# Turning x for the q projection: PE transposes replaced by a DRAM round trip and 32x32 block transposes, from the fourth tile on

## The chip, the cores and the metric

One core of one Trainium2 chip runs the kernel. Its engines are named as in the profile: PE (TensorE, with its weight loads PEld), DVE (VectorE), ACT (ScalarE), POOL (GpSimd) and SP (SyncE, which here only issues DMAs). Each engine works through its own list of instructions in order and waits on semaphores. The metric is the time of one execution on the device in microseconds; less is better.

## The reference

Everything is float32. There are 32 tiles of 128 tokens with 512 features each; a tile attends only to its own 128 context rows (the image part of the context; the text part is empty here). The second half is a feed-forward layer.

```python
def attention_block(x, ctx):                       # x, ctx: (32, 128, 512), 16 heads of 32
    xn = (x - mean(x)) / sqrt(var(x) + 1e-5)
    q = rms_norm(xn @ q_w.T + q_b, norm_q_w)
    k = rms_norm(ctx @ k_img_w.T + k_img_b, norm_k_img_w)
    v = ctx @ v_img_w.T + v_img_b
    a = softmax(q @ k.T / sqrt(32)) @ v            # per head
    return x + tanh(g_xattn) * (a @ o_w.T + o_b)

def feed_forward(x):
    h = normalise(x)
    y = square(relu(h @ up_w)) @ down_w + (h @ expert_w) * sum(top2(h @ gate_w))
    return x + tanh(g_ffn) * (layer_norm(y) * gamma + beta)
```

## The kernel before

The kernel has two phases in one block of instructions: attention, which writes its result tile by tile to a DRAM scratch, and the feed-forward layer, which works on groups of four tiles. The change is in the first.

**Precision.** A float32 product is done on PE as three products of a high and a low part. So every stationary and moving operand is split: ACT copies it to a rounded high part (`cT_hi`, `xnT_hi`, `aT_hi`), and DVE or POOL subtracts that from the original to get the low part (`cT_lo`, `xnT_lo`, `aT_lo`). The helper `mm3` then issues three matmuls for each of the four slices of 128 features. `xnT_hi` and `xnT_lo` are the transposed normalised x: 128 features of a slice on the partitions, tokens along the columns.

**Slots.** `run` calls one function `slot(s, par)` on every engine, for s = -1 to 30, mostly from a hardware loop of two slots per turn (`par` is the parity, which picks one of two buffers); `drain` does the rest. A slot works on four tiles at once: s (scores and softmax), n = s+1 (projections of k, q, v), a = s-1 (turning the probabilities, multiplying with v), o = s-2 (output projection and residual).

**PE's order in a slot** (L367): scores of s; k projection (`BK`) and q projection (`BQ`) of n, the latter behind `dv_xT`, the count of finished `xnT_lo`; three groups of probability transposes; the output projection of o; the fourth group; the turn of kf; the values (L343), whose last quarter waits for ACT's `pT` of group 3; `turn_x` of tile s+2 (L305), four 128x128 transposes of `xn` into the PSUM bank 7 (`BTX`); the turn of qf; the v projection (`BV`). `BTX`, `BQ` and the output projection's `BO` are the same bank, which is why `turn_x` waits for `dv_qb` and `dv_x2`.

**DVE's order in a slot** (L508): `bias_v` (vb = v projection + bias, L496), `lo_xT` (xnT_lo from `BTX`, L444 in the profile), four `maxima` (L466), reciprocals (`inverse`) between ACT's exponentials, kb, `normalise` of tile s+2 (xn, L456), qb, kf, `residual_sum`, the statistics of a later x, `split_values` (aT_lo); in slots 24 to 27 also the statistics of a feed-forward tile.

**ACT's order in a slot** (L690): the exponentials in four groups (L641), each behind its maxima; squares of k and q; the copies `pT` of the four groups (L619); qf; kT; cT_hi; aT_hi; qT; `hi_xT` (xnT_hi from `BTX`); in slots 2 to 21 the high part of a piece of the feed-forward weights.

**POOL's order in a slot** (L825): in slots 3 to 22 first the low part of such a piece, released by vb (L988); four divides of the probabilities (L801); small square roots; the residual plus bias (L823); cT_lo (L788); in slots 24 to 27 the normalisation of a feed-forward tile (L1223).

**SP's order in a slot** (L245): load of xres; load of xin for tile s+4, behind xn of tile s+2; load of cin for s+4, behind ACT's cT_hi and POOL's cT_lo; store of x2; stores and load of weight pieces. All go to one DMA queue.

**The round trip that exists already.** In the feed-forward phase x is turned without PE: `out_blocks` (L1417) stores a tile to DRAM in runs of 32 columns (128 bytes), dealt so that each 32x32 block lies where it must be, `in_blocks` (L1421) loads it back row by row, and `turn_blocks` (L1154, STREAM_TRANSPOSE) transposes each 32x32 block on DVE. There four tiles are stored and loaded one after the other.

Of the kernel before, what the change touches and what calls it, by code (L numbers as in the profile page):

```python
# [5 lines left out]
F32 = mybir.dt.float32  # L6
# [5 lines left out]
P = 128  # L12
D = 512
KT = D // P
# [9 lines left out]
def flamingo_layer(nc, t, out):  # L24
# [8 lines left out]

    x2_dram = nc.dram_tensor("x2_scratch", [NB, P, D], F32, kind="Internal").ap()
    xn_dram = nc.dram_tensor("xn_scratch", [2 * GB, P, D], F32, kind="Internal").ap()
    ring_dram = nc.dram_tensor("ring_scratch", [t["down"].shape[1] // D + KT, 2, P, D], F32, kind="Internal").ap()

    def at_least(eng, sem, value, apart=False):
# [9 lines left out]
    with ExitStack() as whole:  # L48
        def sem(name):
            return whole.enter_context(nc.semaphore(name))  # L50

        def sb(ctx, name, shape, dt=F32):
            return ctx.enter_context(nc.sbuf_tensor(name, shape, dt))
# [40 lines left out]
        with ExitStack() as ctx:  # L94
# [6 lines left out]
            kf, qf = sb(ctx, "kf", [P, D]), sb(ctx, "qf", [P, D])  # L101
            kb, qb = sb(ctx, "kb", [P, D]), sb(ctx, "qb", [P, D])
            xn = sb(ctx, "xn", [P, D])
            bv = sb(ctx, "bv", [P, D])
            tgbo = sb(ctx, "tgbo", [P, D])
            vb = [sb(ctx, f"vb{n}", [P, D]) for n in range(2)]
# [18 lines left out]

            ld_w = [[sem(f"ld_w{n}{k}") for k in range(2)] for n in range(4)]
            ld_bk, ld_bq, ld_bv, ld_bo, ld_n = (sem("ld_" + n) for n in ("bk", "bq", "bv", "bo", "norms"))
            ld_x, ld_c, ld_r = ([sem(f"{s}{n}") for n in range(2)] for s in ("ld_x", "ld_c", "ld_r"))
            wh, wl, wl_late, cst = sem("weights_hi"), sem("weights_lo"), sem("late_weights_lo"), sem("row_consts")
            pe_K, pe_Q, pe_Tx, pe_TP, pe_PV, pe_Tk, pe_Tq, pe_S, pe_O = (  # L130
# [24 lines left out]

            def is_slot(b, n):
                return isinstance(b, int) and b == n

            def probs_taken(eng, a, g):

# [32 lines left out]
            def strip(h):  # L193

                return slice(h * HD, (h + 1) * HD)

            def by_strip(a):

# [13 lines left out]
            def _(sp):  # L212
# [32 lines left out]
                def slot(s, par):  # L245
                    a, n, o = s - 1, s + 1, s - 2
                    if has(a):
                        at_least(sp, dv_x2, a - 1, apart=True)
                        load(a, 1 - par, t["x"], xres, ld_r)
                    if has(s + 4):  # L250
                        at_least(sp, dv_xn, s + 3, apart=True)
                        load(s + 4, par, t["x"], xin, ld_x)
                        at_least(sp, ac_c, s + 3, apart=True)
                        at_least(sp, po_c, s + 3, apart=True)
                        load(s + 4, par, t["ctxT"], cin, ld_c)
                    if has(o):
                        at_least(sp, dv_x2, o + 1, apart=True)
                        sp.dma_start(x2_dram[o], x2[par][:, :]).then_inc(st_x2[par], DMA)
                    if ff.has_half(s - 3):
                        ff.q_store(sp, s - 3, 1 - par)  # L260
                    if ff.has_half(s - 1):
                        ff.q_load(sp, s - 1, 1 - par)
                    if is_slot(s, NB - 9):
                        for m in range(2):
                            sp.wait_ge(st_x2[m], GB // 2 * DMA)
                    if isinstance(s, int) and NB - 9 <= s < NB - 4:
                        ff.load_first(sp, s - (NB - 9))
# [19 lines left out]
            def _(pe):  # L287
# [16 lines left out]

                def turn_x(b):  # L305
                    at_least(pe, dv_qb, b)
                    at_least(pe, dv_x2, b - 3)
                    at_least(pe, dv_xn, b + 1)
                    turn(xn, BTX, pe_Tx)

# [56 lines left out]
                def slot(s, par):  # L367
# [3 lines left out]
                    if has(n):  # L371
                        at_least(pe, po_c, n + 1)
                        mm3(pe, BK, cT[1 - par], wk, ready=split_weight(n, 0)).then_inc(pe_K, 1)
                        at_least(pe, dv_xT, n + 1)
                        mm3(pe, BQ, xT, wq, ready=split_weight(n, 1)).then_inc(pe_Q, 1)
                    if is_slot(s, 0):
                        pe.wait_ge(dv_vb, 1)
# [19 lines left out]
                    if has(a):  # L397
                        for g in range(NG):
                            values(a, 1 - par, g)
                    if has(n + 1) and not is_slot(n, 0):  # L400
                        turn_x(n + 1)
                    if has(n):
                        at_least(pe, ac_qf, n + 1)
# [38 lines left out]
            def _(dve):  # L442
# [9 lines left out]

                def normalise(b, par):
                    at_least(dve, po_rs, b + 1)
                    at_least(dve, pe_Tx, b)
                    dve.tensor_scalar(xn[:, :], xin[par][:, :], mv[:, 0:1], rstd[:, 0:1], ALU.subtract, ALU.mult).then_inc(dv_xn, 1)  # L456

                def lo_xT(b):
                    at_least(dve, ac_xT, b + 1)
                    sub(xnT_lo[:, :], BTX, xnT_hi[:, :]).then_inc(dv_xT, 1)  # L460

                def maxima(b, g):

# [44 lines left out]
                def slot(s, par):  # L508
# [54 lines left out]
                        stats(s + 3, 1 - par)  # L563
                    if has(a):
                        split_values(a)
                    if starting:
                        stats(2, 0)
                    if is_slot(s, 0):
# [48 lines left out]
            def _(act):  # L617
# [1 line left out]
                    return act.activation(dst, src, ACT.Copy)  # L619

                def hi_xT(b):
                    at_least(act, pe_Tx, b + 1)
                    copy(xnT_hi[:, :], BTX).then_inc(ac_xT, 1)

                def hi_ctx(b, par):
                    at_least(act, ld_c[par], parity_count(b, par))
# [1271 lines left out]
```

## Time and profile before

| | |
|---|---|
| median of 3 runs | 1374.52 us (1373.98 to 1375.23) |
| the profiled execution | 1372.42 us |
| its span | 1370.6 us |
| attention: PE alone on the chain of waits | 61.9 to 537 us |
| feed-forward phase | from about 560 us to the end |
| instructions | 27962 |

The profile is of one execution. Its page gives the busy time of each engine, the span in 40 slices, the DMA queues, the chain of work that ended last, the costliest groups of instructions and the DMA issues. The timeline lists instructions by start time, with the idle time before one and what ended it in brackets. An instruction's recorded duration can overlap the next one's start: the distance of two starts tells what an instruction costs on its engine. A stage table gives each engine's busy time within a stretch.

### The profile page before, as it was taken

How to read it: one execution, taken by the hardware profiler on the slowest of the kernel's cores; microseconds unless marked ns; L12 is line 12 of the kernel's file. 1: busy time of each engine (PE TensorE's matmuls, PEld its weight loads, DVE VectorE, ACT ScalarE, POOL GpSimd, SP SyncE). 2: the span in 40 equal slices, each digit the busy share in tenths (PEclk: the TensorE clock that was granted, in tenths of full speed). 3: DMA queues.
4: the chain of work that ended last, by engine and by line, in shares of the span. 5: the costliest groups of instructions: out<-in, count | busy, mean ns of one | idle time of the engine just before them, and what ended most of it. 6: DMA issues, size and time to landing. Idle time of an engine off the chain costs nothing.

```text
span 1370.6 us, 27962 instructions
## 1 busy us (share of the span) xinstructions
PE 1334.5 (97%) x9264; PEld 1139.9 (83%) x9264; DVE 893.7 (65%) x1739; ACT 614.1 (45%) x1891; POOL 524.2 (38%) x671
## 2 busy tenths in 40 slices
PE   6899999999999999999999999999999999999996
PEld 5688888888888888898888888888888888888884
DVE  5555555555555655887776785775775776776764
ACT  4777777777777777532312212322213113223210
POOL 3566666666665776433131131140140140240211
PEclk9999999999999999999999999999999999999998
DMA  6133333333333311448549449458368468367541
GB/s 232 55 99 109 107 107 107 107 107 111 120 113 96 104 63 41 160 140 204 180 147 253 144 154 252 130 154 254 125 164 250 138 168 249 116 177 222 174 144 36
DMA packets 215091, 199.15 MB, mean 145 GB/s; under 512 B 126321, under 2 KB 126449, under 8 KB 215025
## 3 DMA queue, kind: packets, MB, share of 16 engines
q1 hardware_dynamic: 182768, 139.57, 34.9%
q10 hardware_dynamic: 32256, 58.73, 12.8%
q8 instruction: 37, 0.61, 0.2%
q14 instruction: 30, 0.24, 0.1%
HBM read 156.32 MB, written 41.94 MB: 145 GB/s over the span
## 4 chain that ended last, share of the span: by engine, by line
PE 81%; issue 8%; DVE 5%; POOL 1%; ACT 1%; ACTq 0%; DVEq 0%; POOLq 0%
PE bank L75 16%; PE bank L77 16%; PE bank L76 16%; PE wide L76 7%; PE wide L77 7%; PE wide L75 7%; PE bank L340 4%; PE bank L302 3%; PE wide L318 2%; PE wide L352 2%; ACT prob L641 1%; DVE c L1298 1%; POOL yrstd L1790 1%; PE wide L1491 1%; PE wide L1488 1%
## 5 line engine op out<-in xcount | busy, mean ns | idle before, releaser
L1565 ACT ACTIVATE hT_hi<-c 128x512 fp32r<-128x512 f32 x128 | 79.9, 631 | 402.9 <-PE wide L77 210.1
L641 ACT ACTIVATE prob<-wide,nmx 128x128 f32<-128x128 f32 x512 | 182.3, 403 | 103.4 <-DVE nmx L466 100.1
L1797 POOL TENSOR_TENSOR pair<-pair,beta 128x512 f32<-128x512 f32 x28 | 37.5, 1339 | 451.3 <-DMA pair<-x_scratch 451.3
L76 PE MATMUL wide<-wo_lo,hT_hi 128*128 128x512 f32 x512 | 203.3, 397 | 0.0
L77 PE MATMUL wide<-wo_hi,hT_lo 128*128 128x512 f32 x512 | 201.9, 394 | 0.0
L75 PE MATMUL wide<-wo_hi,hT_hi 128*128 128x512 f32 x512 | 201.5, 394 | 0.0
L801 POOL TENSOR_TENSOR prob<-prob,rr 128x512 f32<-128x512 f32 x128 | 138.3, 1081 | 94.9 <-DVE rr L474 92.0
L1643 DVE TENSOR_TENSOR hT_lo<-c,hT_hi 128x512 fp32r<-128x512 f32 x128 | 99.2, 795 | 75.6 <-ACT hT_hi L1565 74.8
L641 ACT ACTIVATION_READ_ACCUMULATOR prob<-wide,nmx 128x1 f32 x512 | 124.0, 242 | 0.0
L77 PEld LDWEIGHTS wide<-wo_hi,hT_lo 128*128 128x128 f32 x512 | 96.1, 188 | 22.7
L75 PEld LDWEIGHTS wide<-wo_hi,hT_hi 128*128 128x128 f32 x512 | 96.2, 188 | 21.5
L76 PEld LDWEIGHTS wide<-wo_lo,hT_hi 128*128 128x128 f32 x512 | 96.1, 188 | 20.6
L75 PE MATMUL bank<-wq_hi,up_hi 128*128 128x256 f32 x384 | 108.6, 283 | 3.1 <-DVE c L1271 3.1
L76 PE MATMUL bank<-wq_lo,up_hi 128*128 128x256 f32 x384 | 107.9, 281 | 0.0
L77 PE MATMUL bank<-wq_hi,up_lo 128*128 128x256 f32 x384 | 107.7, 281 | 0.0
L1298 DVE SCALAR_TENSOR_TENSOR c<-c 128x512 f32<-128x512 f32 x128 | 83.8, 696 | 0.0
L77 PE MATMUL bank<-wv_hi,up_lo 128*128 128x256 f32 x288 | 81.2, 282 | 0.0
L76 PE MATMUL bank<-wv_lo,up_hi 128*128 128x256 f32 x288 | 80.9, 281 | 0.0
L75 PE MATMUL bank<-wv_hi,up_hi 128*128 128x256 f32 x288 | 80.8, 280 | 0.0
L466 DVE TENSOR_REDUCE nmx<-wide 128x4 f32<-128x512 f32 x128 | 79.3, 682 | 0.0
L619 ACT ACTIVATE pT<-bank 128x512 f32<-128x512 f32 x122 | 75.0, 669 | 5.4 <-PE bank L340 4.6
L75 PEld LDWEIGHTS bank<-wq_hi,up_hi 128*128 128x128 f32 x384 | 72.4, 189 | 4.4 <-DVE c L1271 4.4
(226 smaller groups left out, 3548.7 us busy)
## 6 DMA issues: line engine op xcount, KB each, us to landing
wo_hi<-ring_scratch ACTq DMA_DIRECT2D x110, 256.0 KB, 3.7
wo_lo<-ring_scratch ACTq DMA_DIRECT2D x110, 256.0 KB, 4.5
wo_hi<-ring_scratch SPq DMA_DIRECT2D x46, 256.0 KB, 2.7
wo_lo<-ring_scratch SPq DMA_DIRECT2D x46, 256.0 KB, 2.9
fx<-x_scratch SPq DMA_DIRECT2D x36, 256.0 KB
xin<-in_x SPq DMA_DIRECT2D x32, 256.0 KB, 2.6
cin<-in_ctxT SPq DMA_DIRECT2D x32, 256.0 KB, 2.8
xres<-in_x SPq DMA_DIRECT2D x32, 256.0 KB, 4.0
```

Of the source, the lines that this page charges most:

```text
L75: eng.matmul(dst, ah, bh, start=first and k == 0, stop=False)
L76: eng.matmul(dst, ah, bl, start=False, stop=False)
L77: mm = eng.matmul(dst, al, bh, start=False, stop=last and k == n - 1)
L302: mm = pe.transpose(cols(dst, k), cols(src, k), ident[:, :])
L340: mm = pe.transpose(cols(dst, h), prob[par][:, g, h * P:(h + 1) * P], ident[:, :])
L466: dve.tensor_reduce(nmx[:, g * HG:(g + 1) * HG], bank[g].rearrange("p (h k) -> p h k", h=HG), AX.X, ALU.max, negate=True).then_inc(dv_mx, 1)
L619: return act.activation(dst, src, ACT.Copy)
L641: i = act.activation(prob[par][:, g, h * P:(h + 1) * P], cols(bank[g], h), ACT.Exp, bias=nmx[:, n:n + 1], scale=1.0, accum_out=rs[:, n:n + 1])
L801: pool.tensor_tensor(p, p, r, ALU.mult).then_inc(po_p, 1)
L1298: dve.scalar_tensor_tensor(out=cc[:, m, :], in0=cc[:, m, :], scalar=0.0, in1=cc[:, m, :], op0=ALU.max, op1=ALU.mult).then_inc(dv_h, 1)
L1565: return act.activation(dst, src, ACT.Copy)
L1643: dve.tensor_tensor(ff.hT_lo[i % 2][:, :], ff.c[i // 2 % 2][:, i % 2, :], ff.hT_hi[i % 2][:, :].bitcast(F32), ALU.subtract).then_inc(ff.dv ...
```

## The change

From tile 3 on (`XD = 3`, `dealt(b)`), PE no longer turns xn. Instead:

- SP stores `xn` to the scratch `xd_dram` in runs of 32 columns, in front of the load of the next xin, and after the store has landed (`st_xd`) loads the rows back to `x_dealt`, in front of the load of cin.
- DVE transposes the 32x32 blocks of `x_dealt` into `x_turned` (`turn_blocks`), behind `split_values`.
- ACT's `hi_xT` and DVE's `lo_xT` read `x_turned` from SBUF instead of the bank, block by block, and write `xnT_hi` and `xnT_lo` in token order: runs of 32 read side by side, written 4 floats apart (`by_blocks`, `in_order`).
- `normalise` waits until the store of the tile before has landed instead of for PE's turn. The wait on `dv_x2` that guarded the bank in `turn_x` now stands in front of the q projection. ACT's `hi_xT` waits for PE's last q projection.

```diff
+    xd_dram = nc.dram_tensor("xd_scratch", [2, P, D], F32, kind="Internal").ap()
...
+            x_dealt, x_turned = sb(ctx, "x_dealt", [P, D]), sb(ctx, "x_turned", [P, D])
...
+            XD = 3
+            def dealt(b):
+                return not isinstance(b, int) or XD <= b < NB
+            def dealt_count(b):
+                return (b - (XD - 1)) * DMA
...
+            def by_blocks(a):
+                return a[:, :].rearrange("p (c k b) -> p k c b", c=KT, k=KT)
+            def in_order(a):
+                return a[:, :].rearrange("p (k b c) -> p k c b", c=KT, k=KT)
...
 # SP, slot
+                    if dealt(s + 2):
+                        at_least(sp, dv_xn, s + 3, apart=True)
+                        there = xd_dram[par].rearrange("(i b) (c k d) -> (b c) k i d", i=HG, c=KT, k=KT)
+                        sp.dma_start(there, xn[:, :].rearrange("p (k i d) -> p k i d", k=KT, i=HG)).then_inc(st_xd, DMA)
                     if has(s + 4):
                         at_least(sp, dv_xn, s + 3, apart=True)
                         load(s + 4, par, t["x"], xin, ld_x)
+                    if dealt(s + 2):
+                        at_least(sp, st_xd, dealt_count(s + 2), apart=True)
+                        at_least(sp, dv_xt, s + 2 - XD, apart=True)
+                        sp.dma_start(x_dealt[:, :], xd_dram[par]).then_inc(ld_xd, DMA)
+                    if has(s + 4):
                         at_least(sp, ac_c, s + 3, apart=True)
                         at_least(sp, po_c, s + 3, apart=True)
                         load(s + 4, par, t["ctxT"], cin, ld_c)
...
 # PE
                 def turn_x(b):
                     at_least(pe, dv_qb, b)
-                    at_least(pe, dv_x2, b - 3)
                     at_least(pe, dv_xn, b + 1)
                     turn(xn, BTX, pe_Tx)
...
                         at_least(pe, dv_xT, n + 1)
+                        at_least(pe, dv_x2, o)
                         mm3(pe, BQ, xT, wq, ready=split_weight(n, 1)).then_inc(pe_Q, 1)
...
-                    if has(n + 1) and not is_slot(n, 0):
+                    if is_slot(s, 0):
                         turn_x(n + 1)
...
 # DVE
                 def normalise(b, par):
                     at_least(dve, po_rs, b + 1)
-                    at_least(dve, pe_Tx, b)
+                    at_least(dve, pe_Tx, min(b, XD) if isinstance(b, int) else XD)
+                    if not isinstance(b, int) or b > XD:
+                        at_least(dve, st_xd, dealt_count(b - 1), apart=True)
...
                 def lo_xT(b):
                     at_least(dve, ac_xT, b + 1)
-                    sub(xnT_lo[:, :], BTX, xnT_hi[:, :]).then_inc(dv_xT, 1)
+                    if dealt(b):
+                        sub(in_order(xnT_lo), by_blocks(x_turned), in_order(xnT_hi)).then_inc(dv_xT, 1)
+                    else:
+                        sub(xnT_lo[:, :], BTX, xnT_hi[:, :]).then_inc(dv_xT, 1)
+
+                def turn_blocks(b):
+                    at_least(dve, ld_xd, dealt_count(b))
+                    at_least(dve, ac_xT, b)
+                    dve.transpose(x_turned[:, :], x_dealt[:, :]).then_inc(dv_xt, 1)
...
                     if has(a):
                         split_values(a)
+                    if dealt(n + 1):
+                        turn_blocks(n + 1)
...
 # ACT
                 def hi_xT(b):
-                    at_least(act, pe_Tx, b + 1)
-                    copy(xnT_hi[:, :], BTX).then_inc(ac_xT, 1)
+                    if dealt(b):
+                        at_least(act, dv_xt, b - (XD - 1))
+                        at_least(act, pe_Q, b)
+                        copy(in_order(xnT_hi), by_blocks(x_turned)).then_inc(ac_xT, 1)
+                    else:
+                        at_least(act, pe_Tx, b + 1)
+                        copy(xnT_hi[:, :], BTX).then_inc(ac_xT, 1)
```

## Rows read from the trace of the kernel before

**Rows 1.** The page's part 1: busy us, share of the span, instructions.
```profile
PE 1334.5 (97%) x9264; PEld 1139.9 (83%) x9264; DVE 893.7 (65%) x1739; ACT 614.1 (45%) x1891; POOL 524.2 (38%) x671
```

**Rows 2.** Stage table, one slot: length, busy per engine, PEclk, DMA share, GB/s.
```profile
200.00:216.55 16.55, 16.55 (x141) 13.68 (x141) 8.97 (x19) 12.76 (x49) 10.40 (x14) 1.00 0.35 111
```

**Rows 3.** Chain that ended last, attention's score blocks: start us, us, what.
```profile
61.94 1.10 PE wide L318 x32
...
525.43 1.10 PE wide L318 x32
```

**Rows 4.** Timeline, PE, slot 11: start us, us, engine, line, operation, out<-in.
```profile
206.05 1.08 PE L352 MATMUL wide<-pT,vb 128*32 128x128 f32 x32
207.06 0.66 PE L302 MATMUL bank<-ident,xn 128*128 128x128 f32 x4
207.55 0.60 PE L302 MATMUL bank<-ident,qf 128*128 128x128 f32 x4
207.91 0.48 PE L75 MATMUL bank<-wv_hi,eight 128*128 128x512 f32 x1
...
210.85 1.17 PE L318 MATMUL wide<-kT,qT 32*128 32x128 f32 x32
```

**Rows 5.** Timeline, PE, slot 30, which has no x to turn.
```profile
537.12 1.08 PE L352 MATMUL wide<-pT,vb 128*32 128x128 f32 x32
538.13 0.66 PE L302 MATMUL bank<-ident,qf 128*128 128x128 f32 x4
538.54 0.48 PE L75 MATMUL bank<-wv_hi,eight 128*128 128x512 f32 x1
```

**Rows 6.** Timeline, DVE, slots 11 and 12; L444 eight is xnT_lo.
```profile
211.05 0.69 DVE L496 TENSOR_TENSOR vb<-bank,bv 128x512 f32<-128x512 f32 x1 [2.51 <-PE bank L77]
211.65 0.68 DVE L444 TENSOR_TENSOR eight<-bank,eight 128x512 fp32r<-128x512 f32 x1
212.25 2.48 DVE L466 TENSOR_REDUCE nmx<-wide 128x4 f32<-128x512 f32 x4
...
216.16 1.41 DVE L456 TENSOR_SCALAR xn<-xin,mv,rstd 128x512 f32<-128x512 f32 x1
...
224.40 0.69 DVE L444 TENSOR_TENSOR aT_lo<-wide,aT_hi 128x512 fp32r<-128x512 f32 x1 [0.80 <-ACT aT_hi L619]
...
232.59 0.54 DVE L456 TENSOR_SCALAR xn<-xin,mv,rstd 128x512 f32<-128x512 f32 x1
```

**Rows 7.** Timeline, SP's DMA issues of the same slot.
```profile
217.82 0.33 SPq L220 DMA_DIRECT2D xin<-in_x  x1
225.38 0.33 SPq L220 DMA_DIRECT2D cin<-in_ctxT  x1
```

**Rows 8.** Groups of instructions, feed-forward phase: busy us, mean ns, idle before.
```profile
L1154 DVE STREAM_TRANSPOSE c<-fy 128x512 f32<-128x512 f32 x28 | 18.9, 694 | 2.3 <-DMA fy<-xn_scratch 2.3
...
L1137 DVE TENSOR_TENSOR wq_lo<-c,wq_hi 128x512 fp32r<-128x512 f32 x28 | 18.5, 659 | 8.8 <-ACT wq_hi L1133 8.8
...
L1174 DVE TENSOR_TENSOR up_lo<-pair,up_hi 128x1024 fp32r<-128x1024 f32 x3 | 3.7, 1218 | 0.0
```

**Rows 9.** Line L1417, the 56 dealt stores of the feed-forward phase.
```profile
DMA to landing us min/median/max: 3.9/5.5/8.9
```

**Rows 10.** Line L1421, the 56 loads that bring them back.
```profile
DMA to landing us min/median/max: 2.6/5.0/6.8
```

**Rows 11.** Timeline, ACT: pT of group 3, and the first exponential behind the maxima.
```profile
205.72 0.60 ACT L619 ACTIVATE pT<-bank 128x512 f32<-128x512 f32 x1
...
213.05 0.37 ACT L641 ACTIVATE prob<-wide,nmx 128x128 f32<-128x128 f32 x1 [3.25 <-DVE nmx L466]
```

**Rows 12.** Timeline, POOL: ring subtraction, divide, and normalisation of a feed-forward tile.
```profile
211.90 1.29 POOL L988 TENSOR_TENSOR fy<-fx 128x512 fp32r<-128x512 f32 x1 [2.25 <-DVE vb L496]
...
216.24 1.04 POOL L801 TENSOR_TENSOR prob<-prob,rr 128x512 f32<-128x512 f32 x1 [0.31 <-DVE rr L474]
...
458.92 2.10 POOL L1223 TENSOR_SCALAR fx<-fx,fmv,frstd 128x512 f32<-128x512 f32 x1
```

More of the change, by code:

```diff
@@ L127, in flamingo_layer @@
             ld_bk, ld_bq, ld_bv, ld_bo, ld_n = (sem("ld_" + n) for n in ("bk", "bq", "bv", "bo", "norms"))
+            st_xd, ld_xd, dv_xt = sem("st_xd"), sem("ld_xd"), sem("dv_xt")
             ld_x, ld_c, ld_r = ([sem(f"{s}{n}") for n in range(2)] for s in ("ld_x", "ld_c", "ld_r"))
```

## Prediction

> **What bounds the kernel now.** I read the page's shares first: PE is busy for 97% of the span, DVE for 65%, ACT for 45% [rows 1]. That averages two phases, so the stage table comes next. In a slot of the attention loop (16.55 us) PE is busy for all 16.55 us at granted clock 1.00 (its upper level, 2.4 GHz), DVE for 8.97, ACT for 12.76, POOL for 10.40 [rows 2]. The chain of waits agrees: between its first score block at 61.94 us and the last at 525.43 it runs through PE, 28 periods of 16.55 us [rows 3]. These are slots 2 to 29. What PE no longer executes there comes off the end, until something else becomes late. The start-up before and the drain after are not touched.
>
> The profiled execution took 1372.42 us (span 1370.6 and 1.8 around it), the median of the runs is 1374.52. The sum is made against the former; the median is 2.1 higher and moves with it. About 0.2% (2.7 us) is what a measurement of this kernel can tell from no change.
>
> **Part 1, removed: the turns of xn on PE for tiles 3 to 31.** In slot s the turn of tile s+2 lies between the values and the turn of qf. In a normal slot the values start at 206.05, xn's turn at 207.06, qf's at 207.55, the v projection at 207.91 [rows 4]. The difference of the two turns, 0.49 us, overstates the saving, because the turn that comes first behind the values starts with a small gap, whichever it is. Slot 30 shows it: with no xn left to turn, its values start at 537.12, qf's turn at 538.13 and the projection at 538.54 [rows 5]. From values to projection that is 1.42 us against 1.86, so a slot saves 0.44 us. Slots 1 to 29 are 29 turns: 29 x 0.44 = 12.8 us. (Slot 1 waits for ACT, but before its values; its turn lies behind that wait.) The period would be 16.11 us.
>
> The wait on dv_x2 moves from the turn to the q projection. It asks for a residual sum of the slot before, which precedes aT_lo (224.40 in its slot, [rows 6]) and so is long done. I price it at nothing; the projection's 512-column matmuls cover one more semaphore instruction, and if they didn't, it would be a part of the gap of some 0.1 us seen above.
>
> **Part 2, added: a round trip through DRAM.** It starts when xn is done: 216.16 + 1.41 = 217.57 in one parity, 232.59 + 0.54 = 233.13 in the other [rows 6]. SP issues its next DMA 0.25 us behind the first of these, at 217.82 [rows 7]. The trip's end is needed when DVE gets to the block transpose behind aT_lo, at 224.40 + 0.69 = 225.1 [rows 6]. DVE then idles until vb, one period behind 211.05: 227.6 before, 227.15 with PE 0.44 earlier. A block transpose takes 0.69 us, of which about 0.6 shows before the next instruction starts (vb and xnT_lo start 0.60 apart) [rows 6, 8]. So a landing by 226.5 costs nothing: 8.7 us after issue in this parity, 9.7 in the other.
>
> How long is the trip? The feed-forward phase sends the same patterns: 128-byte runs out, whole rows back. Its stores land after 3.9 to 8.9 us (median 5.5) [rows 9], its loads after 2.6 to 6.8 (median 5.0) [rows 10]. There SP issues four stores in a row and then four loads, beside the ring's loads. Here one store goes out with one load of xin behind it, and the DMA share of the slot is 0.35 [rows 2]. So I take the low ends: 3.9 + 2.6 + 0.3 for the wait and the issue between them = 6.8 us, landed at 224.6, before DVE asks. Both ends for the range: 6.5 and 15.7 us. SP's own queue loses nothing: behind the load of x_dealt comes that of cin, which waits for POOL's cT_lo until 225.38 in any case [rows 7], and the store should be down by 221.8.
>
> The transpose itself lies in DVE's idle time (2.0 us from 225.1 to 227.15). ACT's copy to xnT_hi, now released by it, comes about 0.5 us later than before; ACT is next wanted for the exponentials, before which it idles 3.25 us for DVE's maxima [rows 11].
>
> **Part 3, changed: the subtraction that makes xnT_lo.** This is the edit on a tight path: vb at 211.05, xnT_lo at 211.65 (0.68 us), maxima at 212.25 [rows 6], exponentials from 213.05 [rows 11], then ACT without a pause down to pT of group 3, which ends at 205.72 + 0.60 = 206.32 in its slot [rows 11]. PE needs that pT in the last quarter of the values, at 206.05 + 24/32 x 1.01 = 206.81 [rows 4]. From one engine's end to the next one's start goes 0.16 us (vb ends at 211.74, POOL starts at 211.90, [rows 6, 12]). That leaves 0.33. The maxima could start 0.1 earlier too, since the scores end at 210.85 + 1.17 = 212.02 [rows 4]. So a delay of 0.46 us or less is free, and PE waits by the rest.
>
> The new form reads runs from SBUF and writes with a stride of 4 floats. The trace has the reader: wq_lo out of turned blocks, 0.66 us [rows 8]. A strided write of this size it has not. Below: no change, for the instruction is timed by its 512 columns. Above: each column counts twice, as in the row with 1024 columns, 1.22 us [rows 8]. I take the lower end, the row with the same reader and column count. At the upper end the delay is 0.54 us, of which 0.08 reaches PE: 28 x 0.08 = 2.2 us. ACT's copy, doubled, would still end inside its 3.25 us.
>
> The Trainium skill speaks against this edit: *SBUF — State Buffer*, "Door 1: The DMA port swizzle", says that SBUF has 16-byte lines and that an access which moves to a new line pays. A stride of 4 floats does so every time. It gives no price; if the rule holds, the upper end above is its case, and no row of before can show it.
>
> **Part 4, DVE and POOL shut each other out.** Where POOL's divide starts at 216.24, 0.08 us after xn, xn takes 1.41 us instead of 0.54 [rows 6, 12]. The new subtraction reads two operands from SBUF (before: one from PSUM), so I let it be caught the same way. In slots 3 to 22 POOL's ring subtraction starts at 211.90, 0.25 us behind xnT_lo [rows 6, 12]. DVE is first, and POOL would wait some 0.4 us, in front of a divide that itself waits for ACT. No cost. At the ends of slots 25 to 27 POOL normalises a feed-forward tile, for 2.10 us from 458.92 in the first [rows 12], while the xnT_lo of the next slot starts at 211.65 + 15 x 16.55 = 459.9. Held until 461.02 it would be 1.1 us late; PE's 0.44 of lead and about 0.6 by which the block transpose pushes back POOL's input add to that: 2.2, less the free 0.46, times 3 slots = 5.2 us. Or POOL comes so late that DVE is first, and nothing is lost. Between 0 and 5.2 I take 2.3.
>
> The skill's *SBUF — State Buffer*, "Who interferes with whom", says that a VectorE instruction with two SBUF inputs and a GpSimd instruction that reads SBUF exclude each other to their ends. The xn rows, one input, agree with exclusion as such; for two inputs no row I read decides.
>
> **Sum.** -12.8 + 2.3 = -10.5 us. Profiled execution: 1372.4 - 10.5 = 1361.9. Median: 1364.0.
>
> **Rivals.**
> *A, the strided write costs double.* -12.8 + 2.3 + 2.2, and 0.54 more in each of the three slots: -6.7, 1367.8. For and against it: no row has that stride. 18%.
> *B, the trip is slow and sets the period; slower than before.* It closes a loop that leaves PE out: vb, maxima, exponentials, xn, trip, transpose, next vb. From vb to SP's issue it is 217.82 - 211.05 = 6.77, or 233.13 + 0.25 - 227.6 = 5.78; mean 6.28, and 0.6 for the transpose. The loop reaches 16.55 us at a trip of 9.7 us; from there on the kernel loses. With the medians, 5.5 + 5.0 + 0.3 = 10.8, the period is 17.7: 28 x 1.13 = 32 us more, 1406. For it: same pattern. Against it: four at once there, one here. 9%.
> *C, POOL is first in slots 3 to 22.* xnT_lo would end at 211.90 + 1.29 + 0.68 = 213.87 instead of 212.33 [rows 12]: 1.54 late, 1.08 of it on PE, 20 x 1.08 = 21.6, with the rest +11.1, 1385.6. It decides once DVE's lead of 0.25 us is gone. 7%.
> *D, nothing comes of it:* the write costs more than double (0.9 us late takes all 0.44 back), or another wait on PE takes the place of the turn. 1374. Against it: the other engines' busy times stay below 13.5 of 16.1 us. 9%.
>
> **How the numbers follow.** Forecast 57% (its own range 1361 to 1367), A 18%, B 9%, C 7%, D 9%. Faster by over 0.2%: forecast and A, 0.75. Same: 0.09. Slower: 0.16. The range leaves out B and C. Downwards it ends below the full 12.8 us (1361.7), at 1360.5; upwards it takes in A and reaches into D, to 1373.5.
>
> **What would show it.** In the trace after: PE's score blocks 16.1 us apart and no xn transposes behind slot 0; x_dealt landed about 7 us after xn's end; the block transpose right behind aT_lo; xnT_lo at 0.66 us (A: 1.2) and ahead of POOL's ring subtraction (C: behind it); in slots 26 to 28 an xnT_lo of 2 us or more with a short gap in PE's values. It is wrong if vb starts more than 0.2 us after the projection's end in most slots (B), or if PE pauses in the values of every slot (A beyond its size, C, D).

## The result and the profile after

The changed kernel takes 1364.2 us (median of 4 runs, 1364.02 to 1367.62), the kernel before 1374.65 us on the same chip (4 runs, 1373.98 to 1375.23): ratio 0.993, interval 0.9913 to 0.9947. That is 10.5 us less, as forecast. The two profiled executions are nearer to each other, 1372.42 and 1364.38 us (spans 1370.6 and 1362.5), 8.1 us apart: the one of before lay 2.2 us under its median, the one of after on it. What follows accounts for these 8.1 us.

The page's shares and the chain by engine, as in [rows 1]:

```profile
PE 1323.2 (97%) x9148; PEld 1127.5 (83%) x9148; DVE 922.6 (68%) x1768; ACT 624.7 (46%) x1891; POOL 542.8 (40%) x671
```
```profile
PE 83%; issue 5%; DVE 4%; ACT 2%; DMA 1%; POOL 1%; ACTq 0%; POOLq 0%; DVEq 0%
```

PE still sets the pace. DMA now has a place on the chain of waits, with 1%; on the page of before it had none. The stage table of one slot, as in [rows 2] (length, busy time of PE, PEld, DVE, ACT, POOL, then PEclk, DMA share, GB/s), and PE's timeline behind the output projection, as in [rows 4]:

```profile
200.00:216.10 16.10, 16.10 (x138) 13.21 (x137) 10.39 (x19) 13.02 (x49) 10.92 (x13) 1.00 0.51 145
```
```profile
218.64 1.08 PE L380 MATMUL wide<-pT,vb 128*32 128x128 f32 x32
219.65 0.66 PE L331 MATMUL bank<-ident,qf 128*128 128x128 f32 x4
220.06 0.48 PE L76 MATMUL bank<-wv_hi,eight 128*128 128x512 f32 x1
...
223.00 1.17 PE L346 MATMUL wide<-kT,qT 32*128 32x128 f32 x32
```

The turn of qf follows directly on the values. From values to projection it is 220.06 - 218.64 = 1.42 us, the number of slot 30 before [rows 5], and PE is busy in all of the slot at its upper clock level (granted 1.00, 2.4 GHz).

DVE, ACT and POOL in a slot, as in [rows 6, 11, 12], and SP's issues, as in [rows 7] (start us, duration us; idle time before and its releaser in brackets):

```profile
204.47 0.69 DVE L473 TENSOR_TENSOR aT_lo<-wide,aT_hi 128x512 fp32r<-128x512 f32 x1 [0.96 <-ACT aT_hi L660]
205.07 0.70 DVE L499 STREAM_TRANSPOSE x_turned<-x_dealt 128x512 f32<-128x512 f32 x1
207.08 0.69 DVE L535 TENSOR_TENSOR vb<-bank,bv 128x512 f32<-128x512 f32 x1 [1.30 <-PE bank L78]
207.69 1.07 DVE L473 TENSOR_TENSOR eight<-x_turned,eight 128x512 fp32r<-128x512 f32 x1
```
```profile
205.81 1.11 ACT L660 ACTIVATE eight<-x_turned 128x512 fp32r<-128x512 f32 x1 [0.89 <-DVE x_turned L499]
```
```profile
207.93 1.98 POOL L1034 TENSOR_TENSOR fy<-fx 128x512 fp32r<-128x512 f32 x1 [1.64 <-DVE vb L535]
```
```profile
197.88 0.60 SPq L273 DMA_DIRECT2D xd_scratch<-xn  x1
198.75 0.77 SPq L240 DMA_DIRECT2D xin<-in_x  x1
201.34 0.33 SPq L280 DMA_DIRECT2D x_dealt<-xd_scratch  x1
```

The store of the trip is issued at 197.88, the load at 201.34. Over all 29 tiles the stores (L273) and the loads (L280) land after (min, median, max):

```profile
DMA to landing us min/median/max: 3.3/3.3/10.2
```
```profile
DMA to landing us min/median/max: 2.4/2.6/2.9
```

From 197.88 to 201.34 + 2.6 = 203.9 a usual trip takes 6.0 us, and DVE asks at 205.07. The block transpose runs right behind aT_lo, DVE still idles 1.30 us for vb, and the write with a stride takes 1.07 us on DVE and 1.11 on ACT.

The maximum of 10.2 is one tile. A look at the starts of PE's 32 score blocks gives the periods: 12.40, 20.64, then 23 of 16.12, one of 19.91 (slot 25, from 432.56 to 452.47), three of 16.12, 16.17, 16.45. Before they were 12.39, 20.90, 28 of 16.55, 16.12. (Counted so, the values, turns and projection of [rows 4] lie in slot 10; slot 11 begins with the score block at 210.85. Nothing hangs on it.) The way from the third score block (61.8 us in both) to the last, at 541.48 before and 533.45 now, is 8.0 us shorter: 28 x 0.434 = 12.1 us less, 3.8 more in the long slot, 0.4 more in the last two. The feed-forward phase has kept its length: from the last score block to the end of the span it took 829.1 us before and takes 829.1 now.

The long slot on SP, in its turn for tile 26, which is SP's slot 24:

```profile
415.77 2.59 SPq L1060 DMA_DIRECT2D fx<-x_scratch  x4
...
422.50 0.64 SPq L273 DMA_DIRECT2D xd_scratch<-xn  x1
423.19 7.82 SPq L240 DMA_DIRECT2D xin<-in_x  x1
432.72 0.33 SPq L280 DMA_DIRECT2D x_dealt<-xd_scratch  x1
```

The chain of waits there (start us, us, what), the waits (in total, times, longest), and the DMA engines in the middle of it against a usual stretch:

```profile
422.50 10.20 DMA xd_scratch<-xn
432.72 2.57 DMA x_dealt<-xd_scratch
435.31 0.71 DVE x_turned L499
```
```profile
DVE x_turned L499 <- DMA x_dealt<-xd_scratch: 4.6, 1, 4.6
...
PEld bank L76 <- DVE eight L473: 1.9, 1, 1.9
PEld bank L76 <- DVE qb L583: 1.6, 1, 1.6
```
```profile
208.00:210.00 2.00, 2.00 (x13) 1.66 (x10) 2.00 (x4) 0.53 (x3) 1.91 (x1) 1.00 1.00 332
...
426.00:428.00 2.00, 2.00 (x14) 1.69 (x13) 0.76 (x3) 2.00 (x6) 1.55 (x3) 1.00 0.26 98
```

The late block transpose reaches PE in two waits, for xnT_lo at the q projection and for qb at the output projection. This store needed 10.2 us instead of 3.3, and the issue of xin's load behind it 7.8 us instead of 0.8. In front of them in the same queue stand four loads for the feed-forward phase (`load_first`), a megabyte in all, issued at 415.77. From 426 to 430 us, when nothing else seems to have run beside them, the DMA engines were busy for 0.26 of their time, as if 4 of 16 worked, and moved 96 to 98 GB/s. At that rate the megabyte takes some 10 us (an estimate; the landing of these loads is not in the trace). The busiest stretch of the usual slot, from 208 to 210 us, has a share of 1.00 and 332 GB/s.

### The profile page after: what moved, and what is told of

Its sections match the earlier page's. It is cut to its first block, busy times and chain, and to the rows that moved or that the text cites. A ratio compares the mean times of both kernels' runs of the same rounds, so it can differ in the third digit from the quotient of the medians.

```text
span 1362.5 us, 27965 instructions
## 1 busy us (share of the span) xinstructions
PE 1323.2 (97%) x9148; PEld 1127.5 (83%) x9148; DVE 922.6 (68%) x1768; ACT 624.7 (46%) x1891; POOL 542.8 (40%) x671
## 4 chain that ended last, share of the span: by engine, by line
PE 83%; issue 5%; DVE 4%; ACT 2%; DMA 1%; POOL 1%; ACTq 0%; POOLq 0%; DVEq 0%
PE bank L76 16%; PE bank L77 16%; PE bank L78 16%; PE wide L77 8%; PE wide L78 8%; PE wide L76 8%; PE bank L368 3%; PE wide L380 2%; PE bank L331 2%; PE wide L346 2%; ACT prob L687 1%; DMA xd_scratch<-xn 1%; DVE c L1344 1%; PE wide L1537 0%; PE wide L1534 0%
```

## The experiments

My theory after the result: the saving of 0.43 us a slot is PE's alone; the trip and the strided writes are hidden in every slot but one; in that one the trip stands behind the four loads, and it is their pattern (a view whose outermost dimension has 4 entries, `dealt_rows`) that makes them slow. Rivals: the slow store is a matter of bytes; the trip costs something elsewhere too; the strided write, not the trip, holds PE; the two engines' exclusion would have cost time but for the order in which they start. Each kernel is a small edit of the one after, unless it says otherwise.

### The four loads, spread over four slots

```diff
         if n == 0:
             q_stored(sp)
-            for pos in range(GB):
-                load_x(sp, 0, X_ORDER[pos])
+        if n < GB:
+            load_x(sp, 0, X_ORDER[n])
+        if n == 0:
+            pass
         elif n < 3:
```

> The changed kernel, with the four loads of x2 for the first feed-forward group issued one in each of the slots 23 to 26 instead of all four in slot 23. Theory: in slot 24 of the changed kernel the dealt store stood behind these four loads (landing 10.2 us against 3.3 elsewhere) and PE lost 3.8 us once; spread, the store lands in under 5 us, all 28 periods of the score blocks are 16.12 us, and the median is 3.8 lower, about 1360.4. Rival: the queue is simply full with what slot 24 carries and the loss moves to other slots, in pieces; the median stays at 1364.

Measured: 1361.47 us (1360.52 to 1362.59) beside 1373.82, ratio 0.9905, interval 0.9884 to 0.9926. All periods up to the last two are 16.12 us; the stores of the trip land in 3.3 to 3.9 us. In the slot that was long:

```profile
423.06 0.64 SPq L273 DMA_DIRECT2D xd_scratch<-xn  x1
423.74 1.41 SPq L240 DMA_DIRECT2D xin<-in_x  x1
426.87 0.33 SPq L280 DMA_DIRECT2D x_dealt<-xd_scratch  x1
```

The load is issued 3.8 us behind the store instead of 10.2. The four loads in a row were the cause of the long slot.

The same edit in the kernel before, where no trip stands behind the loads:

> The kernel before, with the same spreading of the four x2 loads. Theory: PE has no trip to wait for there, so all periods stay at 16.55 us and the time at 1374.6. Rival: the loads cost the kernel before something too, and part of what the first run gains is not the round trip's; then this run is 1 to 4 us faster than before.

Measured: 1375.09 us (10 runs, 1372.06 to 1376.89), ratio 1.0004, interval 0.9993 to 1.0015, all 28 periods 16.55. The loads cost nothing as long as nobody waits behind them. The gain of the spread belongs to the trip.

### The four loads in plain rows

```diff
-            sp.dma_start(xn[j], dealt_rows(x2_dram[j])).then_inc(ld_x[j], DMA)
+            sp.dma_start(xn[j], x2_dram[j]).then_inc(ld_x[j], DMA)
```

> The changed kernel with the four x2 loads at their old place in slot 23, but reading the rows of a tile in plain order instead of dealt order; the rows of the first four tiles then come in the wrong order, which leaves the amount of work the same. While the dealt loads ran, the DMA share was 0.26 and the rate some 95 GB/s, as if 4 of 16 engines worked. Theory: the pattern of these loads is what blocks the store; with plain rows 1 MB passes in 4 to 5 us, the store of slot 24 lands in under 5 us, 1360.4. Rival: the amount of bytes is what blocks it; nothing changes, 1364.

Measured: 1361.64 us (1360.57 to 1363.14), ratio 0.9906, interval 0.9885 to 0.9927; all periods up to the last two 16.12, the trip's stores land within 4.2 us, the one behind the four loads after 3.7. The stage table while the four loads run:

```profile
420.00:424.00 4.00, 4.00 (x20) 3.27 (x19) 3.49 (x9) 3.15 (x19) 1.04 (x1) 1.00 0.90 281
```

Same bytes, same place in the queue, but a DMA share of 0.90 and 281 GB/s against 0.26 and 98. So it is the pattern and not the number of bytes. (The plain order changes two things at once, the size of the outermost dimension and the order in which rows are read; no run parts them.) The Trainium skill, *DMA: Bandwidth & Descriptors*, "Rules for kernel authors", says that an outermost dimension with fewer than 16 entries keeps the whole DMA to at most that many engines. The share of 0.26 with 4 entries agrees with it, and speaks for the size of the dimension.

### No trip

```diff
-                        sp.dma_start(there, xn[:, :].rearrange("p (k i d) -> p k i d", k=KT, i=HG)).then_inc(st_xd, DMA)
...
-                        sp.dma_start(x_dealt[:, :], xd_dram[par]).then_inc(ld_xd, DMA)
...
-                    dve.transpose(x_turned[:, :], x_dealt[:, :]).then_inc(dv_xt, 1)
+                    dve.transpose(x_turned[:, :], xn[:, :]).then_inc(dv_xt, 1)
```

> The changed kernel without its round trip: neither the store nor the load of the scratch, and DVE transposes the blocks of xn itself, so x comes out in the wrong order; everything else is the same. Theory: the trip costs nothing but the 3.8 us of slot 24, so this run is at 1360.4 with periods of 16.12 us, the same as the run with spread loads. Rival: the trip's DMAs cost a little everywhere (PE waits that are too small to see, a slower feed-forward phase), and this run is under 1359.

Measured: 1363.15 us (1362.03 to 1365.27), ratio 0.9917, interval 0.9895 to 0.9939; periods 16.12, slot 25 with 16.37, the last two 16.20 and 16.40. Taking the trip away gives no shorter period than the trip gives in a usual slot. It costs nothing there; its price in this kernel is the long slot, less the 0.25 us that slot 25 loses even without a trip. The median is 1.7 us above that of the spread loads on the same chip, where I had expected them equal. In the profiles this is not in the slots: the third score block comes 1.5 us later, and the stretch behind the last one is 0.7 us longer.

### The trip alone, PE turning as before

The kernel before with the trip, the block transpose and their waits added and their result left unused.

> The kernel before with the round trip and the block transpose added and not used: PE turns every xn as before, ACT and DVE split x from the bank as before. Theory: the trip costs PE nothing except behind the four x2 loads; DVE is late by what slot 24's landing exceeds, so 27 periods are 16.55 us and one is 19 to 20 us, and the time is 3 to 4 us above the kernel before, 1377 to 1379. Rival: the extra DMA traffic and DVE's transpose cost a little in each slot; then the other periods are above 16.55 too.

Measured: 1376.57 us (10 runs, 1374.77 to 1379.15) beside 1374.88, ratio 1.0012, interval 1.0003 to 1.0022. All periods 16.55 but one of 19.43. So the added DMAs and the transpose cost 1.7 us on the median (0.4 to 3.0 by the interval), less than the 3 to 4 I had expected, and the trace has 2.9 us in the same one slot and nothing in the others.

### Writes side by side instead of strided

```diff
+            def in_rows(a):
+                return a[:, :].rearrange("p (k c b) -> p k c b", c=KT, k=KT)
...
-                        sub(in_order(xnT_lo), by_blocks(x_turned), in_order(xnT_hi)).then_inc(dv_xT, 1)
+                        sub(in_rows(xnT_lo), by_blocks(x_turned), in_rows(xnT_hi)).then_inc(dv_xT, 1)
...
-                        copy(in_order(xnT_hi), by_blocks(x_turned)).then_inc(ac_xT, 1)
+                        copy(in_rows(xnT_hi), by_blocks(x_turned)).then_inc(ac_xT, 1)
```

> The changed kernel, with xnT_hi and xnT_lo written in runs of 32 columns side by side instead of 4 floats apart; tokens of x then come in the wrong order, the amount of work is the same. In the changed kernel ACT's copy takes 1.11 us and DVE's subtraction 1.07. Theory: the stride is the whole of that, so both fall to 0.62 to 0.69 us; and since the later maxima stayed within PE's slack (0.46 us, of which 0.38 was used), the periods stay at 16.12 us, the time within 1 us of the changed kernel's. Rival: reading from SBUF in blocks costs, not the writing; then the durations stay above 1.0.

Measured: 1366.84 us (1364.86 to 1367.35) beside 1375.59, ratio 0.9932, interval 0.9915 to 0.9948. The groups of instructions, first of this kernel, then of the one after (busy us, mean ns, idle before):

```profile
L477 DVE TENSOR_TENSOR eight<-x_turned,eight 128x512 fp32r<-128x512 f32 x26 | 17.7, 682 | 0.0
L664 ACT ACTIVATE eight<-x_turned 128x512 fp32r<-128x512 f32 x26 | 16.4, 632 | 26.0 <-DVE x_turned L503 26.0
```
```profile
L660 ACT ACTIVATE eight<-x_turned 128x512 fp32r<-128x512 f32 x26 | 28.9, 1112 | 26.8 <-DVE x_turned L499 26.8
L473 DVE TENSOR_TENSOR eight<-x_turned,eight 128x512 fp32r<-128x512 f32 x26 | 28.1, 1080 | 0.0
```

The read of x_turned in runs costs nothing; it is in both. On ACT the write with a stride of 16 bytes is the whole of 0.63 to 1.11 us. On DVE the edit changes two things, for xnT_hi, the second operand, is read through the same view as xnT_lo is written: the step from 0.68 to 1.08 us belongs to the strided read and the strided write together, and no run parts them. PE's period stays at 16.12, so the 0.40 us are hidden, and only the last two periods, 16.17 and 16.45 after and 16.12 here, show something.

In those two slots there is a second cost. POOL, ahead of DVE with an addition for the feed-forward phase, holds xnT_lo back. DVE and POOL of the kernel after, slots 29 and 30:

```profile
501.54 1.40 DVE L473 TENSOR_TENSOR eight<-x_turned,eight 128x512 fp32r<-128x512 f32 x1
...
517.71 1.65 DVE L473 TENSOR_TENSOR eight<-x_turned,eight 128x512 fp32r<-128x512 f32 x1
```
```profile
501.27 0.73 POOL L1239 TENSOR_TENSOR c<-fy,c 128x256 f32<-128x256 f32 x1
...
517.68 0.73 POOL L1254 TENSOR_TENSOR tsum<-tsum,fx 128x256 f32<-128x256 f32 x1
```

With the writes side by side xnT_lo takes 1.00 and 1.01 us there instead of 0.68, so POOL holds it back in that run too, and PE loses nothing. Without the stride the 0.4 us are gone. Whether the stride alone would cost them no run shows; in slots 2 to 24, where nothing holds xnT_lo back, it costs nothing. Against the forecast of the run the median is not lower: its start-up was longer (third score block at 64.2 us against 61.8), and its long slot is there as well (19.52). The third score block came at 61.6 to 64.2 us over the profiles of all kernels here, the ones without the change included, and the stretch behind the last score block took 828.6 to 831.3 us, which is why periods are the better reading.

The Trainium skill's rule of 16-byte lines (*SBUF — State Buffer*, "Door 1: The DMA port swizzle"), which I had weighed against this edit, agrees with these four rows. They have one stride only, 16 bytes, and can't show where the cost begins.

### How much room the path has: one subtraction more

```diff
+                        sub(spare[:, :], x_turned[:, :], xnT_hi[:, :])
                         sub(in_order(xnT_lo), by_blocks(x_turned), in_order(xnT_hi)).then_inc(dv_xT, 1)
```

> The changed kernel with one more subtraction of 512 columns on DVE in front of the one that makes xnT_lo; its result goes to a tile that nobody reads. It puts 0.60 us more in front of the maxima. Theory: 0.08 us of the slack in front of the values' last quarter is left, so PE waits 0.5 us in each slot: periods of 16.63 us, 28 x 0.5 = 14 us slower than the changed kernel, 1378. Rival: the slack is larger than I worked out (ACT could catch up while it waits elsewhere), and the periods stay at 16.12.

Measured: 1401.57 us (1399.46 to 1402.71), ratio 1.0184, interval 1.0167 to 1.0201: far over what I had expected. Periods are 17.5 to 17.8 in the slots with POOL's ring subtraction (3 to 22), and 16.47 behind them. DVE and POOL in one slot:

```profile
222.48 0.68 DVE L474 TENSOR_TENSOR spare<-x_turned,eight 128x512 fp32r<-128x512 f32 x1
223.07 2.17 DVE L474 TENSOR_TENSOR eight<-x_turned,eight 128x512 fp32r<-128x512 f32 x1
```
```profile
222.72 1.58 POOL L1036 TENSOR_TENSOR fy<-fx 128x512 fp32r<-128x512 f32 x1 [1.50 <-DVE vb L537]
```

POOL's subtraction, released by vb, came 0.24 us behind the start of `spare`, waited for it and so stood in front of xnT_lo, which took 2.17 us instead of 1.07. That is the exclusion, and with it the maxima come 1.7 us late (0.60 + 1.10) instead of 0.60. Where POOL has no such work, 0.60 us more on DVE cost PE 16.47 - 16.12 = 0.35 us: the room was 0.25 us with the strided write in place. And PE waits elsewhere than I had said (60 to 400 us):

```profile
PEld bank L76 <- DVE qb L585: 27.4, 19, 1.6
```

It waits at the output projection for qb (19 times, 1.4 us on the mean), not in the values for pT, and behind the ring it is the same wait, with 0.3 us. The path that comes next is xnT_lo, maxima, exponentials, reciprocals, xn, qb, output projection.

### POOL first

POOL's ring subtraction released by the v projection instead of by vb, so that it starts ahead of xnT_lo, which makes rival C of the prediction real:

```diff
-                        at_least(pool, dv_vb, s + 1)
+                        at_least(pool, pe_V, s + 1)
```

> The changed kernel with POOL's ring subtraction (slots 3 to 22) released by the end of the v projection instead of by vb, so that it starts 0.85 us earlier, ahead of xnT_lo. Rival C of the prediction: the two exclude each other, xnT_lo is held until POOL's 1.29 us are over, its record grows to 1.7 us or more, the maxima come 0.7 us later, PE waits 0.6 us a slot: 20 periods of 16.7 us, 12 us slower than the changed kernel, 1376. Rival: two SBUF inputs on DVE don't exclude POOL; xnT_lo stays at 1.07 us and the time at 1364.

Measured: 1378.06 us (10 runs, 1375.16 to 1379.81), ratio 1.0015, interval 1.0006 to 1.0025. Periods alternate, 16.12 and 16.93, and are 16.92 to 17.01 in the last six slots of the ring. DVE and POOL in two consecutive slots:

```profile
194.86 1.08 DVE L473 TENSOR_TENSOR eight<-x_turned,eight 128x512 fp32r<-128x512 f32 x1
...
211.07 1.95 DVE L473 TENSOR_TENSOR eight<-x_turned,eight 128x512 fp32r<-128x512 f32 x1
```
```profile
194.90 2.20 POOL L1034 TENSOR_TENSOR fy<-fx 128x512 fp32r<-128x512 f32 x1 [1.21 <-ACT fx L1030]
...
210.80 1.28 POOL L1034 TENSOR_TENSOR fy<-fx 128x512 fp32r<-128x512 f32 x1 [1.16 <-ACT fx L1030]
```

At 194.86 DVE was first by 0.04 us: it took 1.08 us and POOL 2.20. At 211.07 POOL was first by 0.27: it took 1.28 and DVE 1.95. In every slot of the ring in this run the one that starts first runs at its own speed, and the other ends late by about what was left. POOL was not ahead everywhere because it waits for ACT's fx and not, as I had thought, for the v projection alone: that is the releaser in its rows. The rival's mechanism is real and takes back all that the change brings (1378.06 us beside 1375.59 of the kernel before on that chip), although it struck in 13 slots of the ring for 0.8 us each and not in 20 for 1.08.

The order of the recorded starts does not always decide. In slot 25 of both runs with spread loads and of the one with plain rows POOL's normalisation is recorded 0.11 to 0.12 us ahead of xnT_lo, while vb still runs, and yet DVE kept its speed and POOL took 3.01 us instead of the 2.10 of [rows 12]. In the first of them:

```profile
433.73 3.01 POOL L1271 TENSOR_SCALAR fx<-fx,fmv,frstd 128x512 f32<-128x512 f32 x1
433.84 1.08 DVE L473 TENSOR_TENSOR eight<-x_turned,eight 128x512 fp32r<-128x512 f32 x1
```

Why this pair falls the other way than POOL's subtractions and additions do is open. The rule of the Trainium skill (*SBUF — State Buffer*, "Who interferes with whom") that a VectorE instruction with two SBUF inputs and a GpSimd instruction that reads SBUF exclude each other agrees with both pairs of the run.

### A slower trip

Two more dealt stores ahead of the one that counts; the load of x_dealt waits for all three:

```diff
+                        for m in range(2):
+                            away = xe_dram[2 * par + m].rearrange("(i b) (c k d) -> (b c) k i d", i=HG, c=KT, k=KT)
+                            sp.dma_start(away, xn[:, :].rearrange("p (k i d) -> p k i d", k=KT, i=HG)).then_inc(st_xd, DMA)
```

> The changed kernel with two more dealt stores of xn in front of the real one, to a scratch of their own, and the load waits for all three. It lengthens the round trip, which in the changed kernel is 3.3 + 0.15 + 2.5 = 6.0 us from the store's issue. Rival B of the prediction: trip, transpose and the way from vb to the store's issue (7.0 us now) form a loop that sets the period once the trip is over 16.12 - 7.0 - 0.7 = 8.4 us. With 2 to 2.4 us for each more store the trip is 10 to 10.8 us, the period 17.7 to 18.5, and the run some 45 to 67 us slower than the changed kernel, 1410 to 1430. If the loop were not the mechanism, PE would lose only what is over the next wait, or nothing.

Measured: 1399.64 us (1397.77 to 1401.64), ratio 1.0177, interval 1.016 to 1.0194. Periods 17.64 to 17.83 in slots 4 to 17, 16.4 in slots 18 to 23, 23.46 in the long slot. SP and DVE:

```profile
210.47 1.64 SPq L275 DMA_DIRECT2D xe_scratch<-xn  x2
...
217.20 0.34 SPq L284 DMA_DIRECT2D x_dealt<-xd_scratch  x1
...
228.11 1.67 SPq L275 DMA_DIRECT2D xe_scratch<-xn  x2
```
```profile
219.79 0.71 DVE L503 STREAM_TRANSPOSE x_turned<-x_dealt 128x512 f32<-128x512 f32 x1 [2.04 <-DMA x_dealt<-xd_scratch]
220.42 0.65 DVE L539 TENSOR_TENSOR vb<-bank,bv 128x512 f32<-128x512 f32 x1
221.69 1.09 DVE L477 TENSOR_TENSOR eight<-x_turned,eight 128x512 fp32r<-128x512 f32 x1 [0.61 <-ACT eight L664]
```

The trip is 219.79 - 210.47 = 9.3 us; with 0.6 of transpose and 7.7 from vb to the next store it makes 17.6, the distance of the two stores (228.11 - 210.47). Such a sum closes whatever the cause. What shows the loop of rival B are the waits in it: the block transpose waits 2.04 us for the trip, vb follows it without waiting for PE, and the next store's issue waits for xn. The way from vb to the store is longer than the 6.3 I had read before, since the strided write and ACT's copy, now waited for (0.61), are part of it, and xn, which POOL's divide holds, takes 1.20 us there. From slot 18 on, with the ring still running, xn takes 0.55 us and the period falls to 16.4. The mechanism holds; two stores more added 3.3 us to the trip and not the 4 to 5 I had expected, so the run came out below its forecast.

### Both versions again

> The changed kernel itself, for a comparison on one chip with the run below. 1364 to 1366 us.

> The changed kernel with the four x2 loads spread over four slots, again, beside the changed kernel on the same chip. Theory: 3.4 to 3.8 us below it, the length of the one stall. Rival: the two medians of the earlier runs (1364.2 and 1361.5) differ by chance of the start-up and the difference is under 1.5 us.

Measured, five runs each beside 1374.88 (15 runs): the kernel after 1365.76 us (1365.47 to 1369.05), ratio 0.9935, interval 0.9922 to 0.9949; with spread loads 1362.73 (1359.85 to 1363.91), ratio 0.9912, interval 0.9898 to 0.9926. The profile of the first has the long slot at 21.33 us with a store landing after 11.5, that of the second has none. The two sets do not overlap. Spreading the four loads gives 3.0 us more and beats both kernels. The forecast for that difference was 3.4 to 3.8. The stall of the long slot is not one number: over the profiles that have it, with and without other edits, it cost 2.9 to 5.2 us (without the run of three stores).

## Why the prediction came out right, and where it did not

**Part 1, right.** 29 turns at 0.44 us: the slot got shorter by 16.553 - 16.120 = 0.434 us, 28 times. What the turn in slot 1 brought can't be read. That slot took 20.90 us before and 20.64 after, but over all profiles it takes 20.90 to 21.03 with the turn and 20.44 to 21.89 without it. PE idles for ACT there (3.13 us ahead of 53.69 in the kernel after), and its granted clock then falls to 0.50, the lower level of 1.2 GHz; between 58 and 59 us it was still 0.50 where the kernel before had 0.91. The moved wait on dv_x2 cost nothing, as priced.

**Part 2, right in 28 slots, wrong in one.** The trip takes 6.0 us where I took 6.8, well inside the 8.7 that are free, and without it PE's period is the same. The low ends that I took, 3.9 and 2.6, were the right choice: the store lands after 3.3 and the load after 2.6. The step that failed is the sentence that SP's own queue loses nothing and that here one store goes out with one load behind it. True of the slot I read [rows 7], not of the slot in which `load_first` puts four loads in front of the trip. These were in the code and in the trace of before; I looked at one slot and multiplied. The price is 3.8 us in the profiled execution, and it was not in the sum. This one trip took 12.8 us (10.2 + 2.6), inside the upper bound of 15.7 that I had given but over the 8.7 that are free.

**Part 3, wrong end, small effect.** I took the lower end (0.66) for the strided write; it measured 1.07, nearer the upper end of 1.22, and ACT's copy likewise 1.11. My room of 0.46 us on the path let it cost nothing, and it costs nothing but 0.4 us in slots 29 and 30, where POOL's additions hold it back as well. But the room was read off the wrong wait: with the write in place 0.25 us are left, and what comes late is qb at the output projection, not pT in the values. By that (an estimate) a write that cost 0.3 us more would have made every slot pay.

**Part 4, guess not borne out.** I had put +2.3 us, near the middle of 0 and 5.2, for POOL's normalisations of feed-forward tiles holding xnT_lo. In the trace DVE is first at all three places and loses nothing. In slot 26 it leads by 0.25 us:

```profile
453.19 1.10 DVE L473 TENSOR_TENSOR eight<-x_turned,eight 128x512 fp32r<-128x512 f32 x1
```
```profile
453.44 2.81 POOL L1269 TENSOR_SCALAR fx<-fx,fmv,frstd 128x512 f32<-128x512 f32 x1
```

In slots 27 and 28 the lead is 0.06 us (469.30 and 469.36, 485.42 and 485.48). The exclusion as such was rightly described; that it cost nothing here hung on so little that I call it luck. It did strike in slots 29 and 30, where POOL's additions came first and xnT_lo took 1.40 and 1.65 us; the prediction does not have these. In slots 3 to 22 POOL's subtraction takes 2.0 to 2.1 us instead of 1.29 and nobody waits for it, as argued.

**The sum.** By the traces it is -12.1 + 3.8 + 0.4 = -8.0 (rounded), and 0.1 less again from the start-up and the feed-forward phase: -8.1 against the -10.5 on record. The median moved by 10.5 on the first chip and by 9.1 on the one where both were run again, so the agreement to 0.2 us is partly luck of two kinds: a cost of 2.3 that didn't come stands where one of 3.8 did, and the medians of a few runs scatter by a microsecond or two, by the start-up and by the feed-forward phase. What is well founded is the size: 0.43 us times the slots, less one stall.

**The rivals.** A: the write costs 0.4 of the 0.54 us that A gave it, which stays inside the free 0.46, and PE's wait did not follow. B and C: neither happened in this kernel; both mechanisms exist, and the runs with three stores and with POOL first produced them. D: no; PE is busy for all of the usual slot.

What is open: why the start-up varies by up to 2.6 us between executions (the first score block comes at 28.6 to 30.8 us, slot 1 takes 20.4 to 21.9) and the stretch behind the last score block by as much. Kernels with and without the change show both, and I did not look for the cause.

## What to carry to other kernels

Work taken off an engine that is busy for a whole slot came back here in full (0.43 us of a forecast 0.44), until the next wait is reached; the place to read it is a slot that already lacks the work. What replaces it has to be checked in every slot that differs from the usual one, above all for what stands ahead of it in the same DMA queue: here a trip of 6.0 us became one of 12.8 behind four slow loads. Where two engines exclude each other, look at the lead in start times: with 0.06 us it was kept by luck.

## What the hardware showed that I had not expected

- A float32 write of 512 columns with a stride of 16 bytes takes 1.11 us instead of 0.63 on ACT. A subtraction on DVE that writes so and reads one of its operands so takes 1.08 instead of 0.68. Reading blocks in runs of 32 columns takes nothing extra.
- Four loads of 256 KB whose view has 4 entries outermost run at a DMA share of 0.26 and 98 GB/s, and a store behind them in the queue lands after 10.2 us instead of 3.3; even the issue of the next DMA is held, for 7.82 us. Behind the same bytes in plain rows the store lands after 3.7 us.
- A lead of 0.04 us can decide the exclusion of DVE and POOL: 1.08 and 2.20 us with DVE first by that much, 1.95 and 1.28 with POOL first by 0.27. A normalisation on POOL that is recorded 0.11 us ahead lost all the same, 3.01 us instead of 2.10.
